# First layer of an eight-layer model: gates, magnitudes and input projections in another order, the fourth variance's root earlier, the output bias as a one-row product

## The reference

```
z  = layernorm(x);  xh = z @ W_in + b_in                    # 512 features: 256 real, 256 imaginary
gx, ga = sigmoid(blockdiag(xh, W_gx) + b_gx), sigmoid(blockdiag(xh, W_ga) + b_ga)
a  = exp(-8 * ga * softplus(a_real) + i * a_imag * ga)
h  = scan over tokens of a * h + sqrt(1 - a*a) * gx * (xh_re + i * xh_im)
x += [h.re, h.im] @ W_out + b_out
```

## Time and profile before

| what | us |
|---|---|
| median of 3 runs | 5027.12 (5025.49 to 5028.86) |
| the profiled execution | 5025.78 |
| its span (first to last instruction) | 5024.1 |
| first layer, from its first transfer to its last instruction | 7.6 to 343.4 |

### The profile page before, as it was taken

One profiled execution on the slowest core, in us unless ns is written; L12 is line 12 of the kernel. 1 busy time (PEld: TensorE's weight loads), 2 busy tenths in 40 slices (PEclk: granted clock), 3 DMA queues, 4 the chain that ended last, 5 costly groups with the idle time before them and its releaser, 6 DMA issues. The chain is left out here.

```text
span 5024.1 us, 65280 instructions
## 1 busy us (share of the span) xinstructions
PE 4532.5 (90%) x26052; PEld 2544.3 (51%) x26052; DVE 2503.2 (50%) x3810; ACT 1646.6 (33%) x2825; POOL 1704.5 (34%) x1130
## 2 busy tenths in 40 slices
PE   6359997899999999978999859999999989699996
PEld 3124443433333333245666536666666658566663
DVE  7865888367777777852222234444443444512222
ACT  5414443211555556822111123323333210321110
POOL 2000000101888887024555411222222210155553
PEclk9679998999999999988999979999999999799998
DMA  2000000100000000036888740000010033378897
GB/s 75 0 16 7 7 0 31 40 1 1 2 1 2 1 1 1 1 129 182 257 257 258 168 157 24 32 32 32 25 33 32 24 132 105 134 223 257 257 257 198
DMA packets 241716, 425.99 MB, mean 85 GB/s; under 512 B 31504, under 2 KB 119568, under 8 KB 241424
## 3 DMA queue, kind: packets, MB, share of 16 engines
q1 hardware_dynamic: 184080, 279.28, 16.7%
q0 software_dynamic: 57344, 142.64, 11.6%
HBM read 301.73 MB, written 120.13 MB: 84 GB/s over the span
## 5 line engine op out<-in xcount | busy, mean ns | idle before, releaser
L1557 ACT ACTIVATE attc_prob<-attc_ps 128x512 f32<-128x512 f32 x1024 | 547.6, 597 | 299.0 <-PE attc_ps L1473 289.8
L1589 DVE TENSOR_REDUCE attc_peak<-attc_ps 128x1 f32<-128x512 f32 x768 | 490.7, 682 | 204.6 <-PE attc_ps L1481 204.6
L1444 POOL TENSOR_TENSOR attc_acc<-attc_acc,attc_prob 128x2048 f32<-128x2048 f32 x120 | 543.3, 4528 | 40.4 <-ACT attc_prob L1557 26.5
L1481 PE MATMUL attc_ps<-att_k,att_q 32*128 32x512 f32 x1536 | 492.0, 641 | 0.0
L1473 PE MATMUL attc_ps<-att_q,att_k 32*128 32x512 f32 x2048 | 459.7, 589 | 0.0
L2398 POOL TENSOR_TENSOR linb_sq<-linb_osb 128x512 f32<-128x512 f32 x64 | 90.8, 1419 | 847.3 <-ACT linb_osb L2588 847.3
L1493 PE MATMUL attc_ps<-attc_prob,att_v 128*32 128x256 f32 (+1 forms) x3472 | 310.4, 429 | 0.4 <-ACT attc_prob L1557 0.4
L1074 DVE TENSOR_TENSOR_SCAN ssmb_state<-ssmb_decay,ssmb_bu 128x2048 f32<-128x2048 f32 x64 | 280.7, 4413 | 54.2 <-PE ssmb_y_ps L927 29.4
L2072 POOL DMA_INDIRECT residual_rows<-moe2c_ye,moe2w_index x128 | 201.7, 1575 | 230.1 <-DVE moe2c_ye L2195 200.2
L2072 POOL DMA_INDIRECT residual_rows<-moe1c_ye,moe1w_index x128 | 201.5, 1575 | 230.0 <-DVE moe1c_ye L2195 200.0
L2698 DVE SCALAR_TENSOR_TENSOR linb_gated<-linb_osb,linb_norm_w,linb_proj 128x512 f32<-128x512 f32 x64 | 61.3, 957 | 400.4 <-ACT linb_osb L2588 400.4
(11 more groups left out here) (488 smaller groups left out, 8545.8 us busy)
## 6 DMA issues: line engine op xcount, KB each, us to landing
moe1w_wgu<-in_L_ffn_gate_up_proj SPq DMA_DIRECT2D x32, 1536.0 KB
moe2w_wgu<-in_L_ffn_gate_up_proj SPq DMA_DIRECT2D x32, 1536.0 KB
moe1w_wd<-in_L_ffn_down_proj SPq DMA_DIRECT2D x32, 512.0 KB
gated_features<-linb_gated SPq DMA_DIRECT2D x64, 256.0 KB, 2.3
moe2w_wd<-in_L_ffn_down_proj SPq DMA_DIRECT2D x32, 512.0 KB
linc_gt<-gated_features SPq DMA_DIRECT2D x7, 2048.0 KB, 8.6
linb_wt<-in_L_attn_b_qkv_w SPq DMA_DIRECT2D x16, 768.0 KB, 4.8
residual_rows<-residual SPq DMA_DIRECT2D x8, 1024.0 KB, 4.3
```

The source lines that it names most:

```text
L1444: pool.tensor_tensor(to, before, prob[:, U % NP, :, :], ALU.add).then_inc(pool_done, 2 if at % HALF == 1 else 1)
L1481: nc.tensor.matmul(ps[:, take("peak", U, h), :], q[own, f, i * P:(i + 1) * P], k[own, f, b * NB:(b + 1) * NB], start=True, stop=True).then ...
L1557: nc.scalar.activation(prob[:, U % NP, h, :], ps[:, bank_of(("score", U, h)), :], ACT.Exp).then_inc(exp_done, 1)
L1589: V.tensor_reduce(peak[:, w // TT % 2, i % QH, h, b:b + 1], ps[:, bank_of(("peak", U, h)), :], axis=AX.X, op=ALU.max).then_inc(mx_used, 1)
```

## The change

What it does, by engine:

- SP: the gates' weights come in 8 transfers and their biases in 2, weights first; b_out comes as one row.
- POOL: adds nothing to the residual any more, and sets a row of 128 ones.
- PE: groups f = 0, 1 of blocks 0 and 1, then gate_a of r = 0; groups f = 2, 3 of both, gate_a of r = 1; then gate_x; then the weight's transposes and blocks 2 and 3. Each output tile gets a product of the row of ones with the row b_out. In the second half, a tile's bias product and groups 0, 2 go first (after the step "first", the end of `recur` of r = 0), groups 1, 3 after "half" (four tiles) and "done" (four).
- ACT: takes the magnitudes of the next layer's weight as four Abs with an accumulated sum, between two copies of projections; its projections, gates, features and the fourth root stand in other places of the first half; Ln and Exp are preceded by an explicit load of a table set that holds both.
- DVE: magnitudes are gone, the binarized weight takes 9 instructions where it took 8 larger ones; the fourth tiles' statistics come between `angles` of r = 0 and r = 1 and their normalization after `gate_and_unwind` of r = 0; `angles` of r = 0 waits for gate_a of r = 0 alone. The last `recur` is done in two halves of 512 tokens.

```diff
-        fw = temps[:, 0:2, :].rearrange("p s (k f) -> p (s k) f", f=D)
-        bw = temps[:, 8:10, :].rearrange("p s (k f) -> p (s k) f", f=D)
+        bw, fw = xh[:, :, 2 * NB:3 * NB], xh[:, :, 3 * NB:4 * NB]
+        magnitude = spare[:, 0:D]
-        W_AT = TT - 4
+        W_AT = HT
+        GATED = [(j, r, b) for r in range(GT) for j in (1,) for b in range(2)] + [(0, r, b) for r in range(GT) for b in range(2)]
+        GATED += [(j, r, b) for b in (2, 3) for j in range(2) for r in range(GT)]
+        TAKEN = [(b, f) for r in range(GT) for b in range(2) for f in (2 * r, 2 * r + 1)] + [(b, f) for b in (2, 3) for f in range(DT)]
         def out_bank(i):
+            if i >= HT + 4:
+                return g_ps[:, i % 4, :]
 @block.gpsimd
-            pool.wait_ge(out_loaded, 32)
-            for i in range(TT):
-                pool.wait_ge(z_ready, i + 1)
-                pool.tensor_tensor(g.X[:, i, :], g.X[:, i, :], b_out[:, :], ALU.add).then_inc(biased, 1)
+            pool.memset(one_row[:, :], 1.0).then_inc(biased, 1)
 @block.tensor
+            def outputs(i, ks):
+                if 0 in ks:
+                    nc.tensor.matmul(out_bank(i), one_row[:, :], b_out[:, :], start=True, stop=False)
+                for k in ks:
+                    last = nc.tensor.matmul(out_bank(i), xh[:, k, i * P:(i + 1) * P], w_out[:, k, :], start=False, stop=(k == DT - 1))
+            turns(0)
+            pe.wait_ge(w_loaded, 32)
+            inputs(0, (0, 1))
+            turns(1)
+            inputs(1, (0, 1))
+            pe.wait_ge(blocks_loaded, 16 * 10)
+            gate_input(1, 0, 0)
+            gate_input(1, 0, 1)
+            inputs(0, (2, 3))
+            inputs(1, (2, 3))
+            gate_input(1, 1, 0)
+            gate_input(1, 1, 1)
+            for r in range(GT):
+                gate_input(0, r, 0)
+                gate_input(0, r, 1)
+            weight_turns()
+            turns(2)
+            inputs(2, range(DT))
+            turns(3)
+            for b in (2, 3):
+                if b == 3:
+                    inputs(3, range(DT))
...
+            pe.wait_ge(dve_step, after_vector(1, "first"))
+            pe.wait_ge(g_out, len(GATED))
+            for i in range(HT, TT):
+                if i < HT + 4:
+                    pe.wait_ge(y_used, i - 3)
+                outputs(i, (0, 2))
+            for part in range(2):
+                pe.wait_ge(dve_step, after_vector(1, ("half", "done")[part]))
+                for i in range(HT + 4 * part, HT + 4 * part + 4):
+                    outputs(i, (1, 3))
 @block.scalar
+            def weight_magnitudes():
+                act.wait_ge(fw_loaded, 16)
+                for c in range(DT):
+                    if c:
+                        act.wait_ge(magnitudes, c)
+                    A.activation(magnitude, fw[:, c, :], ACT.Abs, accum_out=below[:, c:c + 1]).then_inc(magnitudes, 1)
             def root(t, r):
                 act.wait_ge(dve_step, after_vector(t, f"real{r}"))
+                A.preload_act_table_set("natural_log_exp_and_others")
-            inputs_out(0, range(DT))
+            inputs_out(0, (0, 1))
             features(1)
             root_of_variance(2)
+            inputs_out(1, (0,))
+            weight_magnitudes()
+            inputs_out(1, (1,))
+            act.wait_ge(blocks_loaded, 16 * 10)
+            gate_out(1, 0, 0)
+            gate_out(1, 0, 1)
+            inputs_out(0, (2,))
...
+            A.preload_act_table_set("natural_log_exp_and_others")
             link(A.activation(fall[:, :], a_real[:, :], ACT.Abs))
...
+            inputs_out(0, (3,))
             for t in range(2):
                 sizes(t, 0)
                 if t == 0:
-                    inputs_out(2, (0,))
+                    inputs_out(1, (2,))
                 own_turn(t, 0)
                 if t == 0:
-                    inputs_out(2, (1,))
+                    inputs_out(1, (3,))
+                    gate_out(1, 1, 0)
+                    gate_out(1, 1, 1)
                 sum_turn(t, 0)
+                if t == 0:
+                    for r in range(GT):
+                        gate_out(0, r, 0)
+                        gate_out(0, r, 1)
+                    root_of_variance(3)
+                    weight_features()
                 sizes(t, 1)
                 own_turn(t, 1)
+                if t == 0:
+                    features(2)
                 sum_turn(t, 1)
+                if t == 0:
+                    inputs_out(2, (0, 1))
                 squares(t, 0)
                 if t == 0:
                     inputs_out(2, (2, 3))
                     features(3)
+                    gates_out(2)
                 parts(t, 0)
                 squares(t, 1)
                 if t == 0:
                     inputs_out(3, (0, 1))
                 absolute(t, 0)
                 if t == 0:
                     inputs_out(3, (2, 3))
                 parts(t, 1)
                 root(t, 0)
                 absolute(t, 1)
                 root(t, 1)
+                if t == 0:
+                    gates_out(3)
 @block.vector
             def add_back(i):
                 dve.wait_ge(y_ready, i + 1)
-                dve.wait_ge(biased, i + 1)
             def recur(t, r):
+                halves = 2 if t and r else 1
+                for part in range(halves):
+                    some = slice(part * TH // halves, (part + 1) * TH // halves)
...
+                    if part + 1 < halves:
+                        tell()
-            dve.wait_ge(fw_loaded, 16)
-            link(V.tensor_scalar(magnitude, fw, -1.0, None, ALU.mult))
-            link(V.tensor_tensor(magnitude, magnitude, fw, ALU.max))
-            link(V.tensor_reduce(alpha[:, :], magnitude, axis=AX.X, op=ALU.add))
+            variances(2)
             normalize(2)
+            dve.wait_ge(magnitudes, DT)
-            link(V.tensor_scalar(bw, fw, 0.0, 2.0, ALU.is_ge, ALU.mult))
-            link(V.tensor_scalar(bw, bw, -1.0, None, ALU.add))
             for c in range(DT):
-                link(V.tensor_scalar(bw[:, c, :], bw[:, c, :], alpha[:, c:c + 1], None, ALU.mult))
-            link(V.tensor_tensor(bw, bw, fw, ALU.subtract))
+                link(V.tensor_scalar(bw[:, c, :], fw[:, c, :], 0.0, alpha2[:, c:c + 1], ALU.is_ge, ALU.mult))
+            for c in range(DT):
+                link(V.scalar_tensor_tensor(out=bw[:, c, :], in0=bw[:, c, :], scalar=alpha[:, c:c + 1], in1=fw[:, c, :],
+                                            op0=ALU.subtract, op1=ALU.subtract))
             link(V.tensor_tensor(bw, bw, fw, ALU.add))
-            normalize(3)
             for t in range(2):
-                dve.wait_ge(g_out, 2 * 4 * (t + 1))
+                dve.wait_ge(g_out, len(GATED) if t else gated_by(1, 0, 1))
+                angles(t, 0)
+                if t == 0:
+                    variances(3)
+                    dve.wait_ge(g_out, gated_by(1, 1, 1))
+                angles(t, 1)
+                if t == 0:
+                    dve.wait_ge(g_out, gated_by(0, 1, 1))
                 dve.wait_ge(x_out, 2 * DT * (t + 1))
-                angles(t, 0)
-                angles(t, 1)
                 gate_and_unwind(t, 0)
+                if t == 0:
+                    normalize(3)
...
                 recur(t, 0)
+                tell()
```

More of the change, by code:

```diff
@@ L366, in inputs, with gate_input @@
                     last.then_inc(x_done, 1)
-            def gate_inputs(b):
+            def gate_input(j, r, b):
+                n = GATED.index((j, r, b))
+                pe.wait_ge(x_out, taken_by(b, 2 * r + 1))
+                if n >= 4:
+                    pe.wait_ge(g_out, n - 3)
+                for k in range(2):
+                    last = nc.tensor.matmul(g_ps[:, n % 4, :], wg[:, j, 2 * r + k, :], xh[:, 2 * r + k, b * NB:(b + 1) * NB],
+                                            start=(k == 0), stop=(k == 1))
+                last.then_inc(g_done, 1)
@@ L369, in gate_inputs @@
+            for b in (2, 3):
+                if b == 3:
+                    inputs(3, range(DT))
                 for j in range(2):
                     for r in range(GT):
[L371 to L374, removed]
-                        for k in range(2):
-                            last = nc.tensor.matmul(g_ps[:, n, :], wg[:, j, 2 * r + k, :], xh[:, 2 * r + k, b * NB:(b + 1) * NB],
-                                                    start=(k == 0), stop=(k == 1))
@@ L378, in gate_inputs @@
-                        last.then_inc(g_done, 1)
-            def outputs(i):
+                        gate_input(j, r, b)
+            pe.wait_ge(out_loaded, 32)
+            pe.wait_ge(biased, 1)
+            pe.wait_ge(x_out, DT * TC)
+            pe.wait_ge(zt_ready, TT + DT)
+            pe.wait_ge(dve_step, after_vector(0, "done"))
+            for i in range(HT):
                 if i >= 4:
                     pe.wait_ge(y_used, i - 3)
-                for k in range(DT):
```

(17 more changed lines are left out.)

120 lines of the change are left out of this document (50 added, 70 removed).

## The result

| | before | after |
|---|---|---|
| median of 5 runs, us | 5028.03 (5025.49 to 5028.86) | 5002.31 (4998.74 to 5002.49) |
| ratio | | 0.9948 (0.9933 to 0.9962) |
| span of the profiled execution | 5024.1 | 5000.6 |
| end of the first layer's last statistics | 343.4 | 318.7 |
| from there to the end of the span | 4680.7 | 4681.9 |

The change saves 25.7 us by the medians, and 23.5 us by the spans of the two profiled executions (that of the kernel before was 2.2 us faster than its median). So the gain is in the first layer.

What follows compares the result with a forecast made beforehand. Layers are parted by barriers; the first layer is bound by DVE in its halves and PE in its tail. 11.4 us from the front plus 17.3 from the tail, 28.7, off 5025.8, plus 1.3: 4998 us, range 4991 to 5008.

Steps and rivals of the forecast that it cites:

- The start: First layer's head: `angles` starts at 51.9 where it started at 78.54, 26.6 us of lead.
- ACT's queue: First half: ACT busy without a pause from 56.4, `features(2)` done at 87.7, only then can PE project block 2.
- PE idle before `wind`: First half, a sign of being wrong: DVE starts `wind`, forecast at 137.4, with PE idle before it.
- Behind it: First half after `features(2)`: DVE waits 9.2, 3.1, 5.9 and 4.6 us; `wind` at 137.4, 11.4 us kept.
- The second half: Stays as it was; one load less in its `root` saves between 0 and 1.29 us, taken as 0.
- The tail: First layer's end: PE from "first" sets it, 36.8 us; last statistics at 326.1 against 343.4, 17.3 us saved.
- rival (3): Bias products of the output tiles: the one-row product costs double, giving 5005 us; chance 0.06.
- (1): First half: stalls in ACT's and PE's chain eat the whole lead; front gives 0 to 5 us, 5004 to 5010; chance 0.16.
- (2): First half: lead kept whole if PE's block 2 is ready in time; 26.6 + 17.3 gives 4983 us; chance 0.05.
- (4): PE stays at 1.2 GHz in front and tail: 5062 us, chance 0.03; tail alone about 3 us slower, chance 0.03.
- (5): First half on ACT: each of seven table switches drains, leaving 2.4 us of the lead, 5007 us; chance 0.02.
- (6): `root` and `fall`: Exp still loads its own table, each 1.3 us longer, 5001 us; within the forecast's 0.65.

Runs made afterwards that it cites:

- the control: The changed kernel as it is, run once more beside the combined kernel: 5004.00 us, ratio to before 0.9952.
- two experiments (44.2 and 44.5): Each against the changed kernel: `features(2)` earlier in ACT's queue, 4998.83 us; the weight's magnitudes back on DVE, 5003.5 us.

## Why the prediction was right, point by point

**Right in sign and range**: 4998 forecast, 5002.3 measured, range 4991 to 5008. The sum said 28.7 us and the layer gave 24.7.

- **The start**: `angles` forecast at 51.9, found at 51.73. The weight is ready before `fall`, the magnitudes end on ACT at 41.5 (forecast 41.6), the third transfer of x is issued at 18.4 (11.3 us earlier, "some 13" forecast), and neither sets `angles`. But the reason given for 6.3 of the 26.6 us, the magnitudes on ACT, fell: on DVE they would have ended in time too. The lead is worth what the last of several covered things leaves, not the sum of its parts. That the time is met to 0.2 us is partly luck: the forecast carried over the slow first products of the kernel before, this profile has them too, and in the control, without them, `angles` starts at 49.69.
- **ACT's queue**: `features(2)`'s last copy forecast to end at 87.7, found at 89.1. This step was 1.4 us short. I took four copies at 2.45; the weight's four took 3.2 and block 2's 3.3. PE had been idle 3.3 and 8.4 us, and its transposes ran at 1.2 GHz (granted clock 0.50 from 86.5 to 88.5; 8 records in 1.94 us, against 1.04 at 105.69), and ACT waited 0.7 to 0.8 and 0.3 us for them. I had charged the slow clock to the products and not to the transposes ahead of them. ACT's idle time between 57 and 88 us, which the prediction named as a sign of being wrong, is there, 1.9 us of it. Another such sign, PE idle before `wind`, is there too (PE ends block 3's gates at 135.8, `wind` starts at 138.75), but it would be by the forecast's own times, 127.4 and 6.9 us of gates against 137.4: it tested nothing.
- **Behind it** all fits: from that copy to `mix` 11.6 forecast and 11.6 found, waits 3.1, 5.9 and 4.6 forecast and 3.25, 5.92 and 4.68 found. The wait before `mix` itself was 10.8 in place of 9.2. Kept of the lead: 10.1 in place of 11.4.
- **The second half** is 0.5 shorter than said: the wait for `root` went from 5.1 to 4.59. I took 0 of a bound of 0 to 1.29; the kernel without the early load shows 0.6.
- **The tail**: PE started at "first" without a pause as said, and neither "half" nor "done" held it. It took 40.0 us in place of 36.8. **The term that was mis-sized is the one-row product**, taken as a full one of 0.86: it costs 1.25. Eight times 0.39 is 3.1, and the kernel with 128 rows got 2.9 of it back. That is rival (3) in kind (double) at under half of its price.
- Together: 28.7 - 1.4 + 0.5 - 3.2 = 24.6.

**Rivals.** (1), the lead eaten whole, did not come about, but its reason, ACT's queue, is real: 16.7 of 26.8 us were lost, and another order gives 15.9 back (120.96 against 136.88). (2), the lead kept, is reached by that order. What stood against it was not `features(2)` alone, as the prediction has it: moving that gave 8.3 us, and the rest came with the other work of blocks 2 and 3. (4), PE at 1.2 GHz throughout, is refuted for the changed kernel: clock 0.94 in the tail, and block 3's 32 records take 13.90 us (115.02), as at full clock. In small it is real: the tails of two experiments (44.2 and 44.5) lost 3 us by it. (5), a drain at each table switch, is refuted; ACT of the changed kernel:

```profile
64.21 1.05 ACT L498 ACTIVATE lru_temps<-lru_temps 128x1024 f32<-128x1024 f32 x1
65.27 1.28 ACT L499 ACT_TABLE_LOAD   x1
66.57 1.06 ACT L499 ACTIVATE lru_temps<-lru_temps 128x1024 f32<-128x1024 f32 x1
```

The load starts 0.01 us after the end of the pass before it, and from its start to that of the activation it is 1.30 us. The Trainium skill, "ScalarE: Activation LUTs", section "What ACT_TABLE_LOAD costs", has 1.38 us of drain on top; no row here shows it, and the forecast of ACT's queue, made without it, is off by 1.4 us over seven switches for another reason. (6), a load ahead of Exp all the same, is refuted by the absence of one there.

What stays open: the first 8 products of the program take 9.46 us in the changed kernel's profile and 7.11 in the control's, with `wind` at 138.75 and 136.88. The same kernel does both; of the thirteen profiles five have the long start. The prediction laid it to 1.2 GHz, but the granted clock reads 1.00 from 21 to 31 us in the kernel before, the changed one and the control, so it does not tell why. The experiments with a short start (136.3 to 136.5) were compared with each other. Not tried: `features(2)` moved alone, with ACT's copies of block 2's groups left where they are.

## What to carry to other kernels

A lead at the head of a chain is worth what the next engine's queue lets through: write that queue out item by item up to the next join, as was done here, and then move the item that feeds an idle engine ahead of those that feed a busy one, or move all that nobody waits for behind what somebody does. Keep the operand shapes of consecutive products alike, even by padding with zeros. When PE restarts after a pause, its transposes are slow too, and the engine that copies them waits.

## What the runs showed of the hardware

- **A switch between 1-row and 128-row products** costs about 0.19 us each way, as long as the weight load, which otherwise lies beside the product before (2.96 us a tile against 2.58 with 128 rows).
- **With one-row products the clock tends to stay down longer.** With the bias product doubled, the first two tiles of the tail took 14.84 us with one row and 9.42 with 128; the granted clock was 0.50 for 15 and 5 us. With single ones they took 8.38 to 11.42 us (six profiles) against 7.21 to 7.77 (two), where the switches explain 0.8; the shortest of the one and the longest of the other differ by no more than that. After each pause of PE before output products of this layer, counted in windows of 1 us, the clock was low for 4.8 to 11.5 us with single one-row products (28 pauses, median 6.3) and for 3.9 to 6.2 with 128-row ones (8, median 5.0). The ranges overlap; what makes the spread is open.
- **DVE beside POOL's adds**: a TENSOR_TENSOR of 128x1024 takes 2.17 us in place of 1.23. The Trainium skill, "GPSIMD Engine Reference", section "Specifications", says that GpSimd shares its SBUF interfaces with VectorE and that they contend when VectorE's instruction reads two SBUF operands; this one does, and the row agrees.
- **A sum taken along with an activation** is a second instruction of its own. In the changed kernel, ACT:

```profile
38.55 0.62 ACT L480 ACTIVATE lru_spare<-lru_xh 128x512 f32<-128x512 f32 x1
39.07 0.19 ACT L480 ACTIVATION_READ_ACCUMULATOR lru_spare<-lru_xh 128x1 f32 x1
```

  Together 0.75 us per 512 columns, from start to start.
- **An explicit table load waits where the automatic one ran ahead**. In the kernel before, the load for the first half's second `root` runs at 150.04, and the activation comes only after a wait for DVE. In the changed kernel the load itself starts at 148.87, after 9.03 us of waiting for DVE. Before:

```profile
150.04 1.28 ACT L484 ACT_TABLE_LOAD   x1
158.98 1.06 ACT L484 ACTIVATE lru_temps<-lru_temps 128x1024 f32<-128x1024 f32 x1 [7.66 <-DVEq L570]
```

  After:

```profile
148.87 1.28 ACT L522 ACT_TABLE_LOAD   x1 [9.03 <-DVEq L623]
```
